# Putting a mixture of experts' results together: the gather split between the last expert and the end

## The chip, the cores and the metric

The kernel is one program on one core of a Trainium2 chip. The metric is the device time of one execution in microseconds (us). TensorE (PE) does the matrix products, VectorE (DVE), ScalarE (ACT) and GpSimd (Pool) work on data in the core's own memory, SyncE (SP) only issues transfers. All five run their own instruction streams and meet at semaphores; transfers run on 16 shared DMA engines.

## What is computed

Two layers over 2048 rows of 512 values. The change touches the end of the second one, a mixture of eight experts of which each row uses two:

```python
probs = softmax(xt @ gate_w.T)
top_vals, top_idx = top_k(probs, 2)
top_vals = top_vals / sum(top_vals)
act = silu(einsum('th,efh->tef', xt, w1)) * einsum('th,efh->tef', xt, w3)
expert_out = einsum('tef,ehf->teh', act, w2)
y = einsum('te,teh->th', w_full, expert_out)      # w_full holds the two top_vals of each row
...
g = silu(y)
x = x + s * g                                     # s: the second attention's message
```

The inputs are drawn from a fixed seed. Worked out from the reference, the eight experts get 515, 546, 493, 538, 524, 479, 477 and 524 rows.

## The kernel before

Four stages run one after the other, each a block of five instruction streams with a barrier between them: `first_stage` (weights and first gate), `attention`, `across_batch` (second attention, routing, and the sorting of rows by expert), `experts`, and then `combine`.

**Sorting.** In `across_batch` VectorE finds for every row its two experts and the two places (`s.slots`) that the row takes in a list sorted by expert, in which each expert starts on a multiple of 128. Pool then writes the rows to `rows_by_expert` (`s.xs`) with 32 indirect transfers (16 tiles of 128 rows, 2 places each, L1187). Places that no row takes stay zero: `attention` fills the whole list with zeros first (L1058). The last instructions of VectorE in this stage (L1339 to L1349) make small tables from the counts: which expert a block of 128 belongs to, when its weights are ready.

**Experts.** The sorted list has 39 blocks (`NBLK`), the most that can occur; with these counts 37 hold rows (5, 5, 4, 5, 5, 4, 4, 5 by expert) and the last two are empty but computed all the same. Each block is a step: its rows are turned (L1669), multiplied with two weight matrices (L1681), gated on ScalarE and VectorE (L1568, L1625), turned (L1692) and multiplied with the third (L1704, L1706). In step b PE also finishes block b-1. ScalarE takes the result out of the accumulator (L1580) and stores it to `results_by_row` (`s.ys`, L1582). Pool loads and converts the next expert's weights (L1073, L1093) into one of two places, for even and for odd experts; each place is free once the last block of the expert in it is done. After the last conversion Pool loads into the free place what the end needs, 16 transfers of 512 KB (L1536): the first layer's output `s.x1` and the message `s.messages`.

**Combine.** A stage of its own. For each of 16 tiles Pool gathers the 128 rows of the first and of the second expert (L1763, 32 in all; five tiles of space, so that from the sixth on it waits for `mixed`), ScalarE scales the first by its weight (L1795), VectorE scales and adds the second (L1782), ScalarE applies silu (L1803), VectorE multiplies by the message (L1777) and adds the first layer's output (L1778), SP stores the tile (L1809). ScalarE works one tile ahead.

What sets the order is the program text of each engine and the semaphores; there is no scheduler.

## Time and profile before

| | us |
|---|---|
| median of 3 runs | 1499.13 (1498.78 to 1500.48) |
| the profiled execution, own time | 1501.16 |
| its span (first to last instruction) | 1499.2 |
| from the end of the last matrix product (1442.4) to the end of the span | 56.8 |

Of the span PE is busy 90%, VectorE 47%, ScalarE 38%, Pool 41%. The row of PE in 40 slices of 37.5 us tells where it is not: in the first slice, in two or three slices around the middle (`across_batch`, from 750 to 880 us), and in the last two slices (`combine`). A group of instructions is named by its line in the kernel, the engine and the operation; "[... <-X]" behind a line of the timeline is how long the engine had been idle and what ended that.

### The profile page before, as it was taken

The page shows a single profiled execution, that of the slowest core. Times are in us where ns is not written, and L with a number is a line of the kernel's source. Part 1 is how long each engine was busy: PE and PEld are TensorE (multiplying, and loading weights), DVE is VectorE, ACT ScalarE, POOL GpSimd, SP SyncE. Part 2 cuts the span into 40 slices and gives each one's busy share as a digit, 9 for nine tenths or more (in the row PEclk, how much of TensorE's full clock was granted, in tenths as well). Part 3 has the DMA queues.
Part 4 walks back from the last instruction along what each step waited for, and adds up shares of the span by engine and source line. Part 5 has one row for each costly group of instructions (what it writes and reads, how often), then busy time and mean ns, then how long its engine had stood idle before and what let it go on. Part 6 is the DMA issues. An engine that isn't in the chain of part 4 may idle for free. (4 is left out here: it accounts for less than half of the span.)

```text
span 1499.2 us, 24968 instructions
## 1 busy us (share of the span) xinstructions
PE 1349.1 (90%) x7870; PEld 1149.3 (77%) x7871; DVE 699.4 (47%) x1617; ACT 565.9 (38%) x1775; POOL 615.0 (41%) x516
## 2 busy tenths in 40 slices
PE   6989899999999999999877579999999999999940
PEld 6934487878787878888547469999999999999930
DVE  6352376666676766666447332223222222232237
ACT  3421276655556656666534221212212111122124
POOL 0020155444444545454325445172662617451135
PEclk9889999999999999999878689999999999999985
DMA  8035720000000000000015566273772728555247
GB/s 290 1 84 143 277 93 15 15 14 14 14 14 14 14 25 17 14 14 15 7 58 177 195 225 187 99 247 109 238 243 96 268 72 289 171 169 182 72 126 258
DMA packets 67068, 171.47 MB, mean 114 GB/s; under 512 B 6448, under 2 KB 15040, under 8 KB 66704
## 3 DMA queue, kind: packets, MB, share of 16 engines
q0 software_dynamic: 25776, 98.73, 19.9%
q1 hardware_dynamic: 35632, 61.95, 12.9%
q10 hardware_dynamic: 5616, 10.23, 1.9%
q8 instruction: 25, 0.41, 0.1%
q14 instruction: 19, 0.16, 0.0%
HBM read 125.26 MB, written 45.61 MB: 114 GB/s over the span
## 5 line engine op out<-in xcount | busy, mean ns | idle before, releaser
L1681 PE MATMUL bank<-expert_weights,rows_t 128*128 x1872 | 359.4, 347 | 1.8 <-DVE rows_t L1613 1.6
L1681 PEld LDWEIGHTS bank<-expert_weights,rows_t 128*128 128x128 f32 x1872 | 340.8, 189 | 5.8 <-issue 2.6
L958 ACT ACTIVATE room<-bank,room 128x256 f32<-128x256 f32 (+1 forms) x512 | 208.9, 415 | 114.0 <-DVE room L891 113.9
L986 POOL TENSOR_TENSOR room<-room 128x1024 f32<-128x1024 f32 (+1 forms) x128 | 187.9, 1468 | 120.1 <-DVE room L868 120.1
L742 PE MATMUL bank<-room 96*128 (+2 forms) x1024 | 189.1, 327 | 0.0
L1625 DVE TENSOR_TENSOR x_keep<-x_keep,bank 128x400 f32<-128x400 f32 x78 | 44.5, 571 | 304.2 <-ACT x_keep L1568 302.9
L1093 POOL TENSOR_TENSOR expert_weights<-x_keep,expert_weights 128x1600 fp32r<-128x1600 f32 (+2 forms) x49 | 160.2, 3270 | 54.9 <-DMA expert_weights<-w 54.6
L742 PEld LDWEIGHTS bank<-room 96*128 96x128 f32 x1024 | 159.1, 191 | 13.7 <-issue 0.4
L1704 PE MATMUL bank<-expert_weights,act_t 128*128 x702 | 165.6, 389 | 1.0 <-ACT act_t L1573 1.0
L993 POOL TENSOR_TENSOR room<-room 128x256 f32<-128x256 f32 x128 | 93.2, 728 | 173.5 <-DVE room L932 172.2
L1704 PEld LDWEIGHTS bank<-expert_weights,act_t 128*128 128x128 f32 x702 | 131.5, 188 | 25.6 <-issue 1.3
L1568 ACT ACTIVATE x_keep<-bank 128x400 f32<-128x400 f32 x78 | 39.3, 504 | 295.1 <-PE bank L1681 295.1
L891 DVE TENSOR_REDUCE room<-bank 128x4 f32<-128x1024 f32 (+1 forms) x128 | 120.9, 945 | 8.3 <-PE bank L742 8.3
L753 PE MATMUL bank<-ident_sb,room 128*128 128x128 f32 x768 | 116.5, 276 | 7.2 <-POOL room L986 3.7
L753 PEld LDWEIGHTS bank<-ident_sb,room 128*128 128x128 f32 x768 | 92.3, 141 | 32.6 <-issue 23.6
L709 PE MATMUL bank<-wq_parts,q_latent_parts 128*128 128x384 f32 x384 | 101.6, 373 | 5.8 <-DVE room L932 3.1
L781 PE MATMUL bank<-wo_parts,out_latent_parts 128*128 128x512 f32 x384 | 95.4, 405 | 8.1 <-DVE room L932 6.6
L958 ACT ACTIVATION_READ_ACCUMULATOR room<-bank,room 128x1 f32 x512 | 102.3, 200 | 0.0
L781 PEld LDWEIGHTS bank<-wo_parts,out_latent_parts 128*128 128x128 f32 x384 | 72.4, 192 | 29.5 <-issue 12.0
L907 DVE COPY probs_t<-bank 128x512 f32<-128x512 f32 x128 | 86.9, 679 | 4.7 <-PE bank L753 4.7
L930 DVE TENSOR_TENSOR room<-bank,consts_sb 128x384 f32<-128x384 f32 x128 | 70.4, 550 | 35.0 <-PE bank L709 34.9
L975 ACT ACTIVATE room<-bank 96x512 f32<-96x512 f32 x128 | 75.0, 586 | 26.2 <-PE bank L722 26.2
(231 smaller groups left out, 1773.4 us busy)
## 6 DMA issues: line engine op xcount, KB each, us to landing
x_keep<-w POOLq DMA_DIRECT2D x28, 800.0 KB, 5.0
expert_weights<-w POOLq DMA_DIRECT2D x28, 800.0 KB, 6.5
x_keep<-w POOLq DMA_DIRECT2D x14, 768.0 KB, 6.0
expert_weights<-w POOLq DMA_DIRECT2D x14, 768.0 KB, 7.7
rows_by_expert<-room SPq DMA_DIRECT2D x1, 9984.0 KB, 29.0
x_keep<-rows_by_expert SPq DMA_DIRECT2D x39, 256.0 KB, 4.0
results_by_row<-x_keep ACTq DMA_DIRECT2D x39, 256.0 KB, 4.6
room<-wo SPq DMA_DIRECT2D x16, 512.0 KB, 5.8
```

What stands on the lines that cost most here:

```text
L709: last = nc.tensor.matmul(psum(6)[:, 0:4 * KC], qs[:, of_q, qt], Wq[:, of_w, 4 * KC * u:4 * KC * (u + 1)], start=(i == 0), stop=(i == 2))
L742: last = nc.tensor.matmul(ps[:, w * hh:w * hh + w], QT[0:KC, qt, h], s.KT[0:KC, ds(b * SEQ, w)], start=False, stop=True, skip_group_check= ...
L753: last = nc.tensor.transpose(psum(5 - kt)[:, P * hh:P * hh + P], Pr[:, m % 4, hh, P * kt:P * kt + P], ident)
L781: last = nc.tensor.matmul(psum(6), OT[:, of_o, P * i:P * i + P], s.Wo[:, of_w, i], start=(p == 0 and i == 0), stop=(p == 2 and i == 7))
L891: v.tensor_reduce(nb[:, par], scores_bank(m)[:, 0:4 * w].rearrange("p (h k) -> p h k", h=4), AX.X, ALU.max, negate=True).then_inc(bias_rea ...
L907: v.tensor_copy(PT[:, pt_slot(two[1], 0)], psum(5)).then_inc(p_out, 1)
L958: last = sc.activation(Pr[:, m % 4, hh, 0:w], scores_bank(m)[:, w * hh:w * hh + w], ACT.Exp, bias=nb[:, par, hh:hh + 1], accum_out=sm[:, p ...
L986: g.tensor_tensor(pr, pr, rs[:, one[1] % 2].unsqueeze(2).broadcast_to([P, 4, w]), ALU.mult).then_inc(normed, 1)
L993: nc.gpsimd.tensor_tensor(q, q, qrot[:, m % 2], ALU.add).then_inc(q_added, 1)
L1093: return s.nc.gpsimd.tensor_tensor(low, raw, high, ALU.subtract)
L1681: last = mm(psum(2 * hf + w)[:, 0:HF], xgT[:, par, of_x, P * k:P * k + P], W[:, ds(off + (of_w * SLOT + (k * 2 + w) * FF + hf * HF), HF)], ...
L1704: mm(psum(7), actT[:, of_a, P * t:P * t + P], W[:, ds(off + (of_w * SLOT + W13 + t * D), D)], start=(i == 0 and t == 0), stop=False)
```

## The change

- The two places of a row are now kept in rising order: `slots[..., 0]` is the smaller, so the expert of lower number, `slots[..., 1]` the higher. The two weights are swapped to match, with eight small instructions on VectorE at the end of `across_batch`; five more work out how many stores of results must have landed before the last expert starts and when it ends (`s.landed`).
- `combine` is gone; its work stands at the end of the `experts` block. After converting the last expert's weights, Pool waits until the results of blocks 0 to 31 have landed, gathers the lower expert's rows of all 16 tiles (none of them can be the last expert), and loads the message. Then it waits until the results of block 36 have landed and gathers the higher expert's rows into sixteen separate places, made of what is left of the free weight place, the staging space and row buffers.
- ScalarE scales the lower rows, six tiles before the last block's result and the others one per tile. VectorE does three passes per tile as before.
- The first layer's output is no longer loaded early by Pool. SP loads it tile by tile, four tiles ahead of its use, between the stores of the output.
- `results_by_row` is now filled with zeros too, in `attention`, right behind the other list: another transfer of 9984 KB. Pool waits for both before it sorts.
- The semaphores of `first_stage` are given back and used again; Pool clears 46 of them at the start of `attention`.

Pool's stream from its last conversion on, at the end of `experts` (and in `combine` before); `late` is the free weight place, `room`, `kept` and `x_keep` are other space, a name behind "waits" is a semaphore. Before:

```order
L1093 TENSOR_TENSOR expert_weights<-x_keep,expert_weights 32x512 [waits high_in0,raw_in0]
L1529 TENSOR_LOAD tables
L1529 ISA x2
L1536 DMA kept<-x_after_layer 128x2x512 [waits y_done]
L1536 DMA kept<-layer_attention 128x2x512
...
L1757 UNCONDITIONAL_BRANCH [waits barrier_Pool_Activation_PE_DVE_SP_gather]
L1763 DMA room<-results_by_row,tables 128x512 x10
L1763 DMA room<-results_by_row,tables 128x512 [waits mixed]
L1763 DMA room<-results_by_row,tables 128x512
```

Now:

```order
L1107 TENSOR_TENSOR expert_weights<-x_keep,expert_weights 32x512 [waits lora_scaled,raw_in0]
L1590 TENSOR_LOAD tables
L1590 ISA x2
L1590 TENSOR_LOAD tables [waits y_stored0]
L1590 ISA x2
L1595 DMA late<-results_by_row,tables 128x512 [waits y_stored1]
L1595 DMA late<-results_by_row,tables 128x512 x15
L1603 DMA late<-layer_attention 128x2x512 x8
...
L1595 DMA late<-results_by_row,tables 128x512 [waits y_stored1]
L1595 DMA late<-results_by_row,tables 128x512 x6
L1595 DMA x_keep<-results_by_row,tables 128x512 x8
L1595 DMA x_keep<-results_by_row,tables 128x512 [waits rows_turned]
```

The barrier between the stages is gone from this stream, sixteen gathers stand ahead of the last blocks, and none of the other sixteen waits for VectorE.

ScalarE's stream around the last block's result. Before, where the results of the last block are followed by the barrier:

```order
L1803 ACTIVATE room<-room 128x512 [waits mixed]
L1795 ACTIVATE room<-room,tables 128x512 [waits c_done,rows_got1]
L1803 ACTIVATE room<-room 128x512 [waits mixed]
L1795 ACTIVATE room<-room,tables 128x512 [waits c_done,rows_got2]
L1803 ACTIVATE room<-room 128x512 [waits mixed]
```

Now, with the last block's result (L1671) and its store in the middle:

```order
L1664 ACTIVATE act_t<-bank2 128x512 [waits act_turned]
L1697 ACTIVATE late<-late,tables 128x512 [waits lower_in]
L1697 ACTIVATE late<-late,tables 128x512 x5
L1671 ACTIVATE x_keep<-bank3 128x512 [waits y_stored0,y_done]
L1673 DMA results_by_row<-x_keep 128x512 [waits y_out]
L1697 ACTIVATE late<-late,tables 128x512
L1707 ACTIVATE late<-late 128x512 [waits higher_added]
```

The scaling of six tiles moved ahead of the last result, and the first silu (L1707) stands behind it.

VectorE's stream for one tile in the new tail (`k_ready` and `silu_done` are numbers used again, here the landing of a gather and of a load):

```order
L1766 SCALAR_TENSOR_TENSOR late<-x_keep,tables,late 128x512 [waits k_ready,lower_scaled]
L1774 TENSOR_TENSOR late<-late 128x512 [waits c_gated]
L1777 TENSOR_TENSOR late<-late 128x512 [waits silu_done,c_done]
```

against before:

```order
L1782 SCALAR_TENSOR_TENSOR room<-room,tables 128x512 [waits scaled]
L1777 TENSOR_TENSOR room<-room,kept 128x512 [waits c_gated]
L1778 TENSOR_TENSOR kept<-kept,room 128x512 [waits c_dve]
```

The same three passes in the same order; only what they wait for has changed.

The core of the diff:

```diff
@@ build
-        s.kept = sb(ctx, "kept", [P, 2, NT, D])
+        s.first_place = sb(ctx, "late", [P, 2 * SLOT])
         experts(s)
-        s.room(sb(ctx, "room3", [P, 10000]))
-        combine(s)
@@ attention
             nc.gpsimd.memset(zeros, 0.0).then_inc(s.zeros_ready, 1)
+            for of_first_stage in s.done_with:
+                pool.sem_clear(of_first_stage)
...
             sp.dma_start(s.xs.rearrange("(n p) h -> p n h", p=P),
+                         zeros.unsqueeze(1).broadcast_to([P, NBLK, D])).then_inc(s.blank, 16)
+            sp.dma_start(s.ys.rearrange("(n p) h -> p n h", p=P),
                          zeros.unsqueeze(1).broadcast_to([P, NBLK, D])).then_inc(s.blank, 16)
@@ across_batch
-            v.tensor_copy(s.slots, slotf).then_inc(slots_ready, 1)
+            v.tensor_tensor(s.slots[:, :, 0], slotf[:, 0], slotf[:, 1], ALU.min).then_inc(slots_ready, 1)
+            v.tensor_tensor(s.slots[:, :, 1], slotf[:, 0], slotf[:, 1], ALU.max).then_inc(slots_ready, 1)
...
+            step(v.tensor_tensor(swap[:, 0], slotf[:, 0], slotf[:, 1], ALU.is_gt))
+            step(v.tensor_tensor(swap[:, 1], slotf[:, 0], slotf[:, 1], ALU.is_gt))
+            step(v.tensor_tensor(keep[:, 0], slotf[:, 0], slotf[:, 1], ALU.is_lt))
+            step.then(v.tensor_tensor(keep[:, 1], slotf[:, 0], slotf[:, 1], ALU.is_lt))
+            step(v.tensor_tensor(crossed[:, 0], ranked[:, 1], swap[:, 0], ALU.mult))
+            step(v.tensor_tensor(crossed[:, 1], ranked[:, 0], swap[:, 1], ALU.mult))
+            step.then(v.tensor_tensor(keep, ranked, keep, ALU.mult))
+            step(v.tensor_tensor(ranked, keep, crossed, ALU.add))
+            step(v.tensor_copy(until[:, 0:1], starts[:, E - 1:E]))
+            step.then(v.tensor_tensor(until[:, 1:2], starts[:, E - 1:E], n_blocks[:, E - 1:E], ALU.add))
+            step.then(v.tensor_tensor(below, until.unsqueeze(2).broadcast_to([P, 2, NBLK + 1]),
+                                      const("by_parity").unsqueeze(1).broadcast_to([P, 2, NBLK + 1]), ALU.is_gt))
+            step.then(v.tensor_reduce(n_below, below.rearrange("p i (r n) -> p i r n", r=2), AX.X, ALU.add))
+            step(v.tensor_scalar(s.landed, n_below, 16.0, 16.0, ALU.mult, ALU.add))
@@ experts, Pool
+            blocks_landed(0)
+            for t in range(NT):
+                bring_rows(z[:, t], t, 0, lower_in)
             for q in range(NT // 2):
-                pool.wait_ge(y_done, NBLK - NT // 2 + q)
-                for i, rows in enumerate((s.x1, s.messages)):
-                    pool.dma_start(s.kept[:, i, 2 * q:2 * q + 2],
-                                   rows[2 * P * q:2 * P * q + 2 * P, :].rearrange("(t p) n -> p t n", p=P)).then_inc(
+                pool.dma_start(S[:, 2 * q:2 * q + 2],
+                               s.messages[2 * P * q:2 * P * q + 2 * P, :].rearrange("(t p) n -> p t n", p=P)).then_inc(
+                                   s.kept_in, 16)
+            pool.wait_ge(s.converted, 1 + (E - 1) * NCH)
+            blocks_landed(1)
+            for t in range(NT):
+                if t == NT - 1:
+                    pool.wait_ge(x_turned, NBLK)
+                bring_rows(higher[t], t, 1, higher_in[t])
@@ experts, SP
+            for t in range(NT):
+                if t + X1 < NT:
+                    sp.wait_ge(summed, t + 1)
+                    sp.wait_ge(x1_in[t % X1], 16 * (t // X1 + 1))
+                    bring_x1(t + X1)
+                sp.wait_ge(done, 2 * t + 2)
+                sp.dma_start(s.out[P * t:P * t + P, :], z[:, t]).then_inc(stored, 16)
@@ experts, ScalarE
+            act.wait_ge(lower_in, 16 * NT)
+            for t in range(SCALED_FIRST):
+                scale(t)
             result(NBLK, 1, False)
+            for t in range(NT):
+                if t + SCALED_FIRST < NT:
+                    scale(t + SCALED_FIRST)
+                act.wait_ge(summed, t + 1)
+                sc.activation(z[:, t], z[:, t], ACT.Silu).then_inc(gated, 1)
@@ experts, VectorE
+            add_higher(0)
+            for t in range(NT):
+                if t + 1 < NT:
+                    add_higher(t + 1)
+                dve.wait_ge(gated, t + 1)
+                v.tensor_tensor(z[:, t], z[:, t], S[:, t], ALU.mult).then_inc(done, 1)
+                dve.wait_ge(done, 2 * t + 1)
+                dve.wait_ge(x1_in[t % X1], 16 * (t // X1 + 1))
+                v.tensor_tensor(z[:, t], z[:, t], x1_at[t], ALU.add).then_inc(done, 1)
```

## Rows read from the trace of the kernel before

**Rows 1.** The page: the chain that ended last, by line, in shares of the span.

```profile
POOL room L1763 2%; DMA room<-results_by_row,tables 1%; DVE room L1782 0%; DVE kept L1778 0%; DVE room L1777 0%; ACT room L1795 0%; POOLq L1756 0%; PEldq L1756 0%
```

**Rows 2.** A stretch: length, PE, PEld, DVE, ACT, POOL busy, PE clock, DMA share, GB/s.

```profile
1440.00:1499.20 59.20, 2.39 (x11) 1.65 (x9) 32.64 (x48) 20.56 (x33) 33.35 (x32) 0.56 0.70 217
```

**Rows 3.** Timeline, last block and first tile: start, length, engine, line, [idle before].

```profile
1437.04 0.60 ACT L1573 ACTIVATE act_t<-bank 128x512 fp32r<-128x512 f32 x1 [0.43 <-PE bank L1692]
...
1438.73 0.29 DVE L1637 TENSOR_TENSOR act_t<-bank,act_t 32x128 fp32r<-32x128 f32 x1
...
1442.42 0.60 ACT L1580 ACTIVATE x_keep<-bank 128x512 f32<-128x512 f32 x1 [4.78 <-PE bank L1706]
1443.05 0.35 ACTq L1582 DMA_DIRECT2D results_by_row<-x_keep  x1
1446.24 1.03 POOL L1763 DMA_INDIRECT room<-results_by_row,tables  x1 [22.39 <-PEq L1756]
...
1451.10 0.72 ACT L1795 ACTIVATE room<-room,tables 128x512 f32<-128x512 f32 x1 [8.08 <-DMA room<-results_by_row,tables]
```

**Rows 4.** The end's instructions by line: duration in ns min/median/max, first, last start.

```profile
L1763 POOL DMA_INDIRECT room<-results_by_row,tables x32: 942/1022/1467, 1446.2 to 1488.0; - x32
L1795 ACT ACTIVATE room<-room,tables x16: 721/722/722, 1451.1 to 1492.6; 128x512 f32<-128x512 f32 x16
...
L1803 ACT ACTIVATE room<-room x16: 612/612/631, 1454.4 to 1494.1; 128x512 f32<-128x512 f32 x16
```

**Rows 5.** Timeline, the last tiles on VectorE.

```profile
1493.35 0.75 DVE L1782 SCALAR_TENSOR_TENSOR room<-room,tables 128x512 f32<-128x512 f32 x1
1494.02 0.69 DVE L1777 TENSOR_TENSOR room<-room,kept 128x512 f32<-128x512 f32 x1
...
1494.74 0.69 DVE L1778 TENSOR_TENSOR kept<-kept,room 128x512 f32<-128x512 f32 x1
1495.35 0.68 DVE L1777 TENSOR_TENSOR room<-room,kept 128x512 f32<-128x512 f32 x1
1496.07 0.69 DVE L1778 TENSOR_TENSOR kept<-kept,room 128x512 f32<-128x512 f32 x1
```

**Rows 6.** Timeline: Pool's last conversion; the stores of blocks 31 and 36.

```profile
1329.95 4.74 POOL L1093 TENSOR_TENSOR expert_weights<-x_keep,expert_weights 128x1536 fp32r<-128x1536 f32 x2 [1.98 <-DMA expert_weights<-w]
...
1351.70 0.35 ACTq L1582 DMA_DIRECT2D results_by_row<-x_keep  x1
...
1422.81 0.36 ACTq L1582 DMA_DIRECT2D results_by_row<-x_keep  x1
```

**Rows 7.** Transfers issued from 1350 to 1352: count, KB, us to landing.

```profile
results_by_row<-x_keep ACTq DMA_DIRECT2D x1, 256.0 KB, 2.4
```

**Rows 8.** Timeline: the start of attention on Pool; and a register instruction's ns.

```profile
167.25 0.52 POOL L1037 MEMSET room<- 128x512 f32 x1 [83.29 <-POOLq L286]
169.83 0.73 POOL L993 TENSOR_TENSOR room<-room 128x256 f32<-128x256 f32 x1 [2.06 <-DVE room L932]
...
L1706 PEldq FUSED_REGOPS  x18: 46/46/46, 1203.3 to 1439.3; - x18
```

**Rows 9.** Timeline: the small table instructions at the end of across_batch.

```profile
798.72 0.17 DVE L1285 TENSOR_TENSOR room<-room 128x16 f32<-128x16 f32 x1
798.93 0.25 DVE L1286 RECIPROCAL room<-room 128x16 f32<-128x16 f32 x1
...
875.57 37.91 SPq L1543 DMA_DIRECT2D x_keep<-rows_by_expert  x6
```

**Rows 10.** Timeline: ScalarE and PE at the end of Pool's scatter.

```profile
849.85 0.60 ACT L1229 ACTIVATE room<-bank 128x512 f32<-128x512 f32 x1 [20.33 <-remote]
...
850.50 3.78 PE L1431 MATMUL bank<-room 128*128 128x128 f32 x16 [11.28 <-ACT room L1229]
```

**Rows 11.** The page's transfers, and SP's next load after the zeros.

```profile
rows_by_expert<-room SPq DMA_DIRECT2D x1, 9984.0 KB, 29.0
...
239.33 0.36 SPq L1045 DMA_DIRECT2D gate_tiles<-gates  x1
```

137 lines of the change are left out of this document (67 added, 70 removed).

## The prediction, made before the change was run

> **What bounds the kernel now.** I read the page first. The chain of work that ended last lies wholly in the combine stage: Pool's gathers L1763, transfers, and a little of each pass on VectorE and ScalarE [rows 1]. Then the table by stretch: in the last 59.2 us PE works 2.39 us, VectorE 32.64, ScalarE 20.56, Pool 33.35, and the DMA engines 0.70 of the time at 217 GB/s [rows 2]. So everything behind the last matrix product is an end of its own, and PE, which sets the pace before it, is not in it. The timeline shows how it starts: ScalarE takes out the last result from 1442.42 to 1443.02, the first gather begins at 1446.24 behind the barrier, and the first tile reaches ScalarE only at 1451.10 [rows 3]. From there 32 gathers follow from 1446.2 to 1488.0 [rows 4]: (1488.0 - 1446.2) / 31 = 1.35 us each, 2.7 us per tile. VectorE needs less: in the one place where it works without a wait, the starts of the passes lie 0.67 (L1782 to L1777), 0.72 (L1777 to L1778, which depends on it) and 0.61 us (L1778 to the next) apart [rows 5], 2.00 us per tile. ScalarE needs 0.72 + 0.61 = 1.33 us [rows 4]. **Pool's issue of gathers bounds the end, VectorE is next.** The last pass ends at 1496.07 + 0.69 = 1496.76 [rows 5] and the span at 1499.2: 2.44 us for the last store.
>
> **The gathers of the lower rows.** Pool is free from 1329.95 + 4.74 = 1334.7 [rows 6]. Block 31's results are issued at 1351.70 [rows 6] and such a store lands in 2.4 us [rows 7], so 16 gathers of 1.35 us run from about 1354.5 to 1376, and eight message loads behind them. This lies beside PE's steps with 80 us to spare. Its cost beside PE I put at nothing; what it is if that cover is gone is the slower rival below. What also goes from this time are eight transfers of 512 KB for the first layer's output, which waited for nobody.
>
> **The gathers of the higher rows.** They wait for block 36, not for the last block: by the counts of the reference the last two of the 39 blocks hold no rows. Block 36's store is issued at 1422.81 [rows 6] and lands near 1425.5; with two table reads on Pool I start at 1426.5. Sixteen gathers of 1.35 us are issued by 1448. The first tile needs its rows at 1439, the last at about 1473, so none is late. If all 39 blocks held rows they would start near 1446, land by 1451 and cost some 5 us; that is a matter of the data and I leave it at zero.
>
> **What is late next.** VectorE finishes its work for the last block at 1438.73 + 0.29 = 1439.02 and ScalarE the same at 1437.64 [rows 3]. ScalarE then scales six tiles (about 0.63 us from start to start, 0.72 the last): until 1441.5. VectorE adds two higher tiles and stops, since the first silu stands on ScalarE behind the last block's result. That result waits for PE until 1442.42, its store is issued until 1443.40 [rows 3], one more scaling takes 0.63 and silu 0.61: 1444.7. Here VectorE starts and does not stop again if nothing else is late: 16 tiles of 0.72 + 0.61 for the two last passes and 14 remaining first passes of 0.67 are 21.3 + 9.4 = 30.7 us, to 1475.4. With the same 2.44 us for the last store the span would end at 1477.8. The gain of the end is **1499.2 - 1477.8 = 21.4 us**. ScalarE's 1.33 us per tile hides behind VectorE's 2.00. SP's load of the first layer's output for tile t+4 is issued when tile t-1 is done, some 10 us before use. The transfers per tile are 256 KB in and 256 KB out per 2.0 us, 262 GB/s. The end of before moved 217 GB/s on average at a DMA share of 0.70 [rows 2], which at a full share would be 310. That is close, but below it; only the last gathers, until about 1450, come on top.
>
> **Costs elsewhere.** (1) VectorE, end of across_batch: 13 small instructions more. Starts of such instructions are 0.21 us apart when the second waits for the first [rows 9], and I take 0.09 without that wait (the 0.17 us of a duration less the 0.08 of overlap that the 0.75 us pass shows against its 0.67 us step in [rows 5]). Six wait at 0.21 to 0.27, seven do not: 6 x 0.23 + 7 x 0.09 = 2.0; I take **1.9 us**. They are in full on the path: SP loads the first rows at 875.57 [rows 9] as soon as VectorE lets the barrier go. (2) One instruction more ahead of the sorting: 0.1 us. (3) Pool clears 46 semaphores between its memset, ended at 167.77, and its first sum at 169.83, where it had been idle 2.06 us [rows 8] and where PE takes up the sum at once. No row shows what clearing costs. From below: nothing, if 46 of them fit into the 2.06 us (up to 45 ns each); from above, 0.30 us each, the pause between two of Pool's gathers (1.35 less their median 1.02), which makes 13.8 - 2.06 = 11.7 us. The nearest row in kind is a register instruction of 46 ns on PE's sequencer [rows 8]: 2.1 us, over the idle time by less than 0.1. I take **0.3**. (4) The second fill with zeros: the first takes 29.0 us [rows 11] from shortly after the memset's end at 167.77 [rows 8], the second would last until about 227, and SP's next load is at 239.33 [rows 11]. Nothing waits for it before the sorting, over 500 us later: zero.
>
> Of (3) the Trainium skill has a figure: "Runtime: NRT & Kernel Launch", section Instruction fetch mechanics, gives a sequencer some 20 cycles per instruction as the least, and "Advanced Engine Details and Errata", Clock Domains, 1.2 GHz for Pool's. An estimate from these pages is 46 x 20 / 1.2 GHz = 0.8 us, well inside the idle time, and the sum would be 0.3 us less; no run here shows it yet.
>
> **The sum.** -21.4 + 1.9 + 0.1 + 0.3 = -19.1 us. Against the profiled execution's span of 1499.2 this is 1480.1, its own time 1501.16 would be 1482.1. The profiled execution lies 2.0 us above the median of the runs, 1499.13, so for the median I forecast **1480 us**, a ratio of 0.987. A difference of under 0.2%, 3 us, is about what a measurement of this kernel can't tell from none.
>
> **Rivals.**
> *A, late code or transfers in the end (+10 us, 1490).* In the sorting stage ScalarE stood 20.33 us and PE 11.28 us, both until Pool's 32 scatters were through [rows 10], with nothing named that they waited for: something that each engine needs came late while Pool's indirect transfers ran. In the new kernel the second run of gathers, 1426.5 to 1448, lies over PE's last product and the start of the tail. If the last result came only behind these gathers, first silu would move from 1444.7 to about 1454, and the end with it: +10. For it speaks that row; against it that in the combine stage of before 32 gathers ran in an even 1.35 us each with ScalarE and VectorE busy 20.56 and 32.64 us beside them [rows 2, 4], with no stop of 10 us. If the DMA engines were the bound, at 217 GB/s instead of 262, 7.3 MB from 1444.7 on would take 34 us instead of 31: a milder form, +3. Chance 0.17.
> A rule of the Trainium skill speaks against A: "Runtime: NRT & Kernel Launch", Instruction fetch mechanics, has the fetch of code running ahead on a queue of its own and mostly hidden while code runs in sequence. By it A would have no price and the time would stay at 1480; the standing engines in rows 10 are why I don't drop it.
> *B, clearing semaphores is dear (+9, 1489).* The upper bound of (3). Pool's first sum would start up to 11.7 us late, and PE turns it at once, so the whole of attention moves. Chance 0.07.
> *C, the sorting stage moves.* The standstill there depends on where code and transfers meet, and both have shifted by an instruction or two. It can shrink or grow; its 11.28 us bound it both ways: 1469 to 1491, most likely within 5 of the forecast. Chance 0.10, half on each side.
> *D, slower (1503).* Both runs of gathers, each over 20 us, stop PE as the scatter did, by its 11.28 us each: 2 x 11.3 = 22.6, and 1480 + 22.6 = 1503. The place is Pool's gathers at 1354 and 1426 beside PE's steps. It decides from 19.1 us of standstill on. Against it: between the stores of blocks 31 and 36 a step took (1422.81 - 1351.70) / 5 = 14.22 us [rows 6] while Pool brought its 512 KB transfers beside it. Chance 0.05.
> *E, nothing of it (1499).* The change doesn't get its early start, because the wait for landed results holds Pool until the last block. Then 16 gathers (21.6 us) would still be all that stands behind 1443, below VectorE's 31; only the first landing, 5 us, is added: 1485. So even this is no zero. Chance 0.03.
>
> **How the numbers follow.** The forecast, 1476 to 1484, has 0.58. A 0.17, B 0.07, C 0.10, D 0.05, E 0.03. To hold 8 in 10 the range takes in A and B and the near half of C: **1475 to 1491**. Faster by over 0.2% (below 1496): all but D and a sum of A and B, **0.91**; within 0.2%: **0.03**; slower: **0.06**.
>
> **What the new profile would show.** Pool's lower gathers near 1356 (plus the 2.3 us by which all is later) and its higher ones from about 1428 to 1450; no gather behind it. VectorE without waits of over 0.1 us from about 1447 to 1478, 2.00 us per tile, and a chain that ended last made of VectorE's three lines alone. If instead VectorE waits for loads of the first layer's output, the DMA engines are the bound; if for silu, ScalarE. At the start, Pool's first sum at 169.8 to 170.3; every us beyond is B. SP's first load of rows 2 us later against the end of the last store of messages. Steps of 14.2 us on PE between 1354 and 1450 speak against A and D. Wrong altogether would be a VectorE pass that is slower on its new places: 0.1 us more per pass is 4.6 us.

## The result, and the profile after

The changed kernel took **1505.17 us** (median of 5 runs, 1503.72 to 1508.21) against 1499.63 us of the kernel before in the same comparison (1498.78 to 1501.53): a ratio of 1.004, with a 95% interval of 1.0029 to 1.0051. It is slower by 5.5 us where 1480 was forecast, and outside the forecast range of 1475 to 1491. Its profiled execution has a span of 1503.4 us, against 1499.2 before.

The end behaves as forecast. This is the timeline of the kernel after: ScalarE's last result, and where VectorE takes up its 14th and 15th tile (start, length, engine, line, operation, in brackets the idle time before it and what ended it).

```profile
1467.96 0.60 ACT L1671 ACTIVATE x_keep<-bank 128x512 f32<-128x512 f32 x1 [3.56 <-PE bank L1827]
...
1495.48 0.75 DVE L1766 SCALAR_TENSOR_TENSOR late<-x_keep,tables,late 128x512 f32<-128x512 f32 x1
...
1497.47 0.74 DVE L1766 SCALAR_TENSOR_TENSOR late<-x_keep,tables,late 128x512 f32<-128x512 f32 x1
```

From the start of the last result to the end of the span it is 1503.4 - 1467.96 = 35.4 us, before 1499.2 - 1442.42 = 56.8 [rows 3]: 21.3 us less. VectorE goes from tile to tile in 1.99 us (1495.48 to 1497.47) without a wait. So the time was lost ahead of the end. The next fence shows where: the two runs of gathers on Pool, and what ScalarE and TensorE (PE) do beside the first.

```profile
1353.66 1.03 POOL L1595 DMA_INDIRECT late<-results_by_row,tables  x1 [20.90 <-DMA results_by_row<-x_keep]
...
1350.75 0.35 ACTq L1673 DMA_DIRECT2D results_by_row<-x_keep  x1
...
1368.01 0.50 ACT L1659 ACTIVATE x_keep<-bank 128x400 f32<-128x400 f32 x1 [11.93 <-remote]
1376.68 0.60 ACT L1671 ACTIVATE x_keep<-bank 128x512 f32<-128x512 f32 x1 [8.17 <-remote]
1377.45 0.35 ACTq L1673 DMA_DIRECT2D results_by_row<-x_keep  x1
...
1363.95 2.33 PE L1802 MATMUL bank<-expert_weights,rows_t 128*128 x10
1366.56 0.34 PE L1802 MATMUL bank<-expert_weights,rows_t 128*128 x1 [0.28 <-issue]
1367.99 0.43 PE L1802 MATMUL bank<-expert_weights,rows_t 128*128 x1 [1.09 <-issue]
...
1376.44 3.02 PE L1802 MATMUL bank<-expert_weights,rows_t 128*128 x8 [0.92 <-issue]
```

Sixteen gathers go out from 1353.66 on, the last at 1372.53. PE still goes on for 12.9 us. Then its matmuls come one by one, 1.4 or 2.1 us from start to start, with nothing in the profile that they wait for ("issue"), until 1376.44, 3.9 us behind the last gather. ScalarE waits 11.93 and 8.17 us for what the profile can only call "remote". These waits begin before PE slows down: the result that ScalarE takes out at 1376.68 was complete when PE's matmul of L1827 ended at 1364.12, by the trace, 12.6 us earlier. From the store of block 31 to that of block 32 it is 26.7 us (1350.75 to 1377.45), where a step of before took 14.22 [rows 6]. The higher rows do the same to the last two blocks:

```profile
1433.47 0.36 ACTq L1673 DMA_DIRECT2D results_by_row<-x_keep  x1
...
1459.07 0.60 ACT L1671 ACTIVATE x_keep<-bank 128x512 f32<-128x512 f32 x1 [14.43 <-remote]
...
1436.90 1.01 POOL L1595 DMA_INDIRECT late<-results_by_row,tables  x1 [57.56 <-issue]
...
1446.24 0.40 PE L1827 MATMUL bank<-expert_weights,act_t 96*128 x1
...
1459.83 0.42 DVE L1733 CAST act_t<-bank 128x256 fp32r<-128x256 f32 x1 [14.32 <-remote]
...
1460.88 6.81 PE L1825 MATMUL bank<-expert_weights,act_t 128*128 x18 [13.47 <-ACT act_t L1664]
```

Here no matmul is late. The one whose signal ScalarE waits for (L1827) ends at 1446.64, and ScalarE starts at 1459.07, 12.4 us behind it. VectorE's cast at 1459.83 waits for transposes of PE that ended at 1447.41, also 12.4 us earlier. PE meanwhile waits for what ScalarE makes of these transposes. So what comes late in this run is what PE signals, for work that the trace shows as done. The last gather is issued at 1455.77, 3.3 us before it is over.

The table by stretch (length; busy time of PE, PE's weight loads, VectorE, ScalarE, Pool; PE clock, DMA share, GB/s) says how much PE does beside the first run, between the runs, beside the second, and right behind it:

```profile
1353.70:1376.40 22.70, 15.08 (x73) 12.40 (x72) 3.76 (x9) 2.13 (x4) 18.13 (x21) 0.87 0.71 210
1377.00:1434.00 57.00, 57.00 (x304) 53.76 (x303) 15.07 (x36) 11.28 (x21) 2.34 (x4) 0.97 0.27 97
1436.90:1459.10 22.20, 10.51 (x59) 9.42 (x57) 3.11 (x8) 1.63 (x4) 15.24 (x16) 0.85 0.66 190
1460.80:1464.00 3.20, 3.12 (x7) 2.51 (x8) 2.70 (x5) 3.20 (x6) 0.00 (x0) 0.50 0.96 307
```

Between the runs PE is busy 57.00 of 57.00 us; beside them 15.08 of 22.70 and 10.51 of 22.20. When PE goes on behind the second run, after standing for 13.47 us, its granted clock is 0.50, the lower of its two levels (1.2 GHz). The 18 matmuls of the last product then take 6.81 us, where the same 18 of the block before take 4.24 at a clock of 1.00. That is how 12.4 us of late signals become 14.9. The chain that ended last, as far as the profile can follow it, now lies on PE for 37% of the span.

Put together, from landmark to landmark (differences to the kernel before in us):

| stretch | before | after | difference |
|---|---|---|---|
| start to Pool's memset of attention [rows 8] | 167.25 | 163.52 | -3.7 |
| to the first load of rows for the last experts [rows 9] | 708.32 | 713.20 | +4.9 |
| to the store of block 31 [rows 6] | 476.13 | 474.03 | -2.1 |
| to the store of block 36 [rows 6] | 71.11 | 82.72 | +11.6 |
| to the last result on ScalarE [rows 3] | 19.61 | 34.49 | +14.9 |
| to the end of the span | 56.78 | 35.44 | -21.3 |

The 26.5 us of the fourth and fifth row are the first and the second run of gathers, and they are more than the 21.3 that the end gives back. The first three rows together are -1.0.

### The profile page after: what moved, and what is told of

Read it like the earlier page. It is cut to its first block and busy times, and to the rows that moved or that the text cites. A ratio compares the mean times of both kernels' runs of the same rounds, so it can differ in the third digit from the quotient of the medians.

```text
span 1503.4 us, 25070 instructions
## 1 busy us (share of the span) xinstructions
PE 1352.4 (90%) x7870; PEld 1152.7 (77%) x7871; DVE 700.1 (47%) x1631; ACT 565.4 (38%) x1775; POOL 604.7 (40%) x508
## 5 line engine op out<-in xcount | busy, mean ns | idle before, releaser
L1671 ACT ACTIVATE x_keep<-bank 128x512 f32<-128x512 f32 x39 | 23.3, 597 | 166.1 <-PE bank L1827 143.5
```

## The experiments

Unless it says otherwise, an edit is made on the kernel after. Executions of one kernel lie up to 11 us apart, largely by what happens before the last expert (the same result of one block came at 1359.63 in one of these kernels and at 1353.68 in the next, with the same code up to there), so where one profiled execution is read, it is read by lengths of steps and not by its span. Ratios are to the kernel before, run beside; where no ratio is given, the time is that of a single execution.

### Lower rows one at a time

```
             for t in range(NT):
+                if t >= 1:
+                    pool.wait_ge(lower_in, 16 * t)
                 bring_rows(z[:, t], t, 0, lower_in)
```

> The changed kernel, but each of the 16 gathers of the lower expert's rows waits until the one before it has landed; they then take about 4.5 us each and fill the time from 1354 to 1427. Theory 1 (what PE signals comes late only while Pool's indirect transfers follow each other without a pause, at 1.25 us): the step in which they lay, 26.7 us, returns to 14.2 and the whole loses its 12 us of standstill, so about 1493 us by the median of the changed kernel, 1505. Theory 2 (every indirect transfer beside PE costs PE a fixed share, about 12 us / 16 = 0.7 us each): the loss is only spread, steps of 16 us or so, and the time stays at 1505. The second run of gathers is left as it is, with its 14.9 us.

Measured: 1492.26 us (1490.79 to 1497.98), ratio 0.9943 (0.9926 to 0.9959). ScalarE's results and the first gathers in the trace of this kernel:

```profile
1359.63 0.60 ACT L1673 ACTIVATE x_keep<-bank 128x512 f32<-128x512 f32 x1 [3.90 <-PE bank L1829]
1373.89 0.60 ACT L1673 ACTIVATE x_keep<-bank 128x512 f32<-128x512 f32 x1 [3.90 <-PE bank L1829]
...
1363.31 1.03 POOL L1595 DMA_INDIRECT late<-results_by_row,tables  x1 [19.91 <-DMA results_by_row<-x_keep]
1367.06 0.97 POOL L1595 DMA_INDIRECT late<-results_by_row,tables  x1 [2.72 <-DMA late<-results_by_row,tables]
...
1460.71 0.60 ACT L1673 ACTIVATE x_keep<-bank 128x512 f32<-128x512 f32 x1 [9.94 <-remote]
```

With a gather every 3.7 us the step is 14.26 us (1359.63 to 1373.89): the first standstill is gone, with the same 16 gathers beside the same products. The second one, beside the higher rows, is still there (9.94 us). So it is the run back to back that costs, not a gather beside PE.

### Higher rows behind the last result

```
             blocks_landed(1)
+            pool.wait_ge(y_done, NBLK + 1)
```

> The changed kernel, but the gathers of the higher expert's rows start only when PE's last product is done, so that this run lies beside no work of PE. Both theories: the last block's result comes 14.9 us earlier, at about 1453 instead of 1468; the first tile then waits for its rows (about 5 us after that), and VectorE's 32 us follow. 1468 + 35.4 becomes 1453 + 5 + 0.7 + 32.6 + 2.4 = 1494 in span, so about 1495 us, 9 less than the changed kernel. If VectorE and ScalarE stand still beside the gathers too (theory 3: every engine is hit, not just what PE signals), tiles would be held up by 10 us or more and the time is 1505 or above.

Measured: 1499.49 us (1492.85 to 1503.76, 10 runs), ratio 0.9986 (0.997 to 1.0002); expected were 1495, just below the 1495.8 to 1500.6 that this interval makes of 1500.30. A part of the time was lost ahead of the edit: in the profiled execution block 31's result came at 1356.77, 6.8 us later than in the kernel after. The lower run stops its step as before; behind the last result the sixteen gathers go out back to back:

```profile
1356.77 0.60 ACT L1672 ACTIVATE x_keep<-bank 128x512 f32<-128x512 f32 x1 [3.90 <-PE bank L1828]
1383.61 0.60 ACT L1672 ACTIVATE x_keep<-bank 128x512 f32<-128x512 f32 x1 [4.01 <-remote]
...
1460.44 0.60 ACT L1672 ACTIVATE x_keep<-bank 128x512 f32<-128x512 f32 x1 [1.12 <-PE bank L1828]
...
1464.64 0.75 DVE L1767 SCALAR_TENSOR_TENSOR late<-late,tables 128x512 f32<-128x512 f32 x1 [7.62 <-DMA late<-results_by_row,tables]
```

VectorE gets its first tile 4.2 us behind the last result and then keeps 1.99 to 2.00 us per tile beside the run. In this end VectorE passes three instructions for a tile, ScalarE two, and neither is held up.

### Both

> Both edits together. Theory 1: 12 us from the first and 9 to 10 from the second, about 1483 us, below both kernels (before 1499.6, changed 1505.2). Theory 2: only the second edit counts, about 1495. Theory 3: about 1493 to 1505.

Measured: **1483.31 us** (1481.37 to 1486.5), ratio 0.9882 (0.9866 to 0.9899), against an expected 1483. Steps are 14.26 us throughout and the last result starts at 1445.10. Taking the two runs out of PE's way brings back nearly the whole forecast: 1505.2 less 1483.3 is 21.9 of the 26.5 us lost, and of the missing 4.6 some 4 are the wait for the first higher rows behind the last result (39.6 us from the last result to the end of the span, where it was 35.4).

### Plain transfers in the place of the lower gathers

```
-                bring_rows(z[:, t], t, 0, lower_in)
+                pool.dma_start(z[:, t], s.ys[P * t:P * t + P, :]).then_inc(lower_in, 16)
```

The lower rows that reach a tile are then those in order, not the tile's own.

> The changed kernel, but the first run of 16 gathers is 16 plain transfers of the same size, 256 KB, from the same list in order, issued back to back on the same queue (the rows that reach a tile are then not its own). If it is the indirect form of a transfer (Pool reading indices and writing descriptors one row at a time) that holds up what PE signals, the step of 26.7 us returns to 14.2 and the span is about 1491. If it is the amount and rate of data on Pool's queue, or on the DMA engines as a whole, the standstill stays and the span is about 1503.

Measured: 1496.78 us. Sixteen transfers of the same 256 KB from the same queue, in a row:

```profile
L1601 POOL DMA_DIRECT2D late<-results_by_row x16: 538/538/581, 1356.8 to 1364.8; - x16
...
1353.38 0.60 ACT L1671 ACTIVATE x_keep<-bank 128x512 f32<-128x512 f32 x1 [3.89 <-PE bank L1827]
1367.63 0.60 ACT L1671 ACTIVATE x_keep<-bank 128x512 f32<-128x512 f32 x1 [3.89 <-PE bank L1827]
```

They are issued in 8.5 us, more than twice as fast as gathers, and the step is 14.25 us. The same bytes at a higher rate don't stop PE; the indirect form does. A run of direct transfers that lasts as long as the 18.9 us of the gathers was not tried, but eight gathers in 9.8 us, hardly longer than these 8.5, do hold ScalarE up (see the next section). This is the row that the prediction lacked: it had argued from direct transfers.

### Bursts of four, of eight, and half rows (each with the higher rows behind the last result)

```
             for t in range(NT):
+                if t and t % 4 == 0:
+                    pool.wait_ge(lower_in, 16 * t)
                 bring_rows(z[:, t], t, 0, lower_in)
```

> As high_late, but the lower gathers go in bursts of four, each burst waiting until all before it have landed. In the changed kernel what PE signalled first came late some 6 us after a run of gathers had begun, so it may take a length of run. If it does: four gathers at 1.25 us are 5 us, with a pause of some 3 us for the last to land, and no step is longer than 14.3 us. If gathers one behind the other hurt from the first on, each of the four bursts costs some 2 to 3 us, steps of 16 to 17 us.

> The same with bursts of eight, 10 us of gathers without a pause. If a length of run is what counts and it is near 6 us: about 4 us late per burst, so two of the steps near 18 us. If the number of gathers counts, the loss is as with bursts of four.

> As high_late, but the 16 lower gathers in a row take half a row each (256 values, 1 KB, so the same number of indices and rows with half the bytes); the other half of each tile, filled with the same first halves, follows one at a time. If Pool's making of the transfers row by row holds up PE's signals, the step still takes about 26 us while the 16 run. If the bytes moved do, the stop is gone or halved (14.3 to 20 us).

Measured: 1488.14, 1486.43 and 1495.09 us. The time alone would not tell four from eight; the waits on ScalarE do. First the two rows of bursts of eight, then of sixteen gathers of half a row each:

```profile
1365.55 0.51 ACT L1662 ACTIVATE x_keep<-bank 128x400 f32<-128x400 f32 x1 [9.20 <-remote]
1378.33 0.51 ACT L1662 ACTIVATE x_keep<-bank 128x400 f32<-128x400 f32 x1 [7.39 <-remote]
```

```profile
1372.26 0.50 ACT L1668 ACTIVATE x_keep<-bank 128x400 f32<-128x400 f32 x1 [15.51 <-remote]
1378.85 0.60 ACT L1680 ACTIVATE x_keep<-bank 128x512 f32<-128x512 f32 x1 [6.09 <-remote]
```

With bursts of four no wait is "remote", and the steps are 14.26 us. Bursts of eight hold ScalarE up twice, by 3.8 us over the three steps in question (46.6 for 42.8). Half the bytes per gather stop it as long as whole rows do: the two steps concerned take 40.4 us for 28.5, 11.9 more, where whole rows cost 11.6. So the length of a run counts, and the size of its gathers does not. Whether length means the number of gathers or the time that they last is not separated: half rows too are issued 1.25 us apart.

### Free work on PE beside the higher run

On the kernel "both": 192 transposes of the identity behind PE's last product, twelve for each tile, which wait for nothing; ScalarE's silu of a tile waits for its twelve.

```
             down(NBLK - 1, place(NBLK - 1))
+            for t in range(NT):
+                for k in range(12):
+                    last = tr(psum(t % 2)[:, P * (k % 4):P * (k % 4) + P], ident, ident)
+                last.then_inc(pe_beside, 1)
```

> The kernel with both edits, whose end ran its 16 gathers back to back beside VectorE and ScalarE at 2.00 us per tile without a wait. Added: behind its last product PE transposes the identity 12 times per tile (about 1.6 us) and signals, and silu of a tile waits for that signal too. If it is what PE signals that comes late beside such gathers, the end stops: ScalarE waits up to 12 to 15 us for PE until the gathers are through, and the span grows from 1484.7 to about 1495. If only the experts' steps are hit for another reason (their loads, their weights), PE stays ahead and the span stays within 2 us of 1485.

Measured: 1496.81 us. PE in this trace, whose sixteen gathers are issued from 1446.21 to 1465.51, and ScalarE's fifth tile:

```profile
1445.77 8.57 PE L1873 MATMUL bank<-ident_sb 128*128 128x128 f32 x77
...
1459.92 0.37 PE L1873 MATMUL bank<-ident_sb 128*128 128x128 f32 x1 [2.58 <-issue]
...
1469.08 14.32 PE L1873 MATMUL bank<-ident_sb 128*128 128x128 f32 x104 [0.71 <-issue]
...
1469.17 0.63 ACT L1712 ACTIVATE late<-late 128x512 f32<-128x512 f32 x1 [11.50 <-remote]
```

This is the disputed cost by itself. Nothing that PE reads, writes or waits for depends on the gathers, and still it does 77 transposes in 8.57 us (its stop begins 8.1 us behind the first gather), eleven in the next 14.7, and the other 104 in one stretch that starts 3.6 us behind the last gather. The late signals of the kernel after are here too: the twelve transposes of ScalarE's fifth tile are among the 77, the last of them ended at 1452.48, and ScalarE takes the tile up at 1469.17, 16.7 us later.

### The same, gathers in bursts of four

> The control to "pe_tail": the same 192 transposes on TensorE behind its last product, with nothing that they wait for, and the higher gathers in bursts of four that wait for their landing. The transposes take 0.11 us each as in the first 8.57 us of "pe_tail", 21 us in all, so ScalarE's tiles never wait for them if TensorE runs freely. Theory 1 (the run back to back slows TensorE's own issue): TensorE goes through the 192 without single matmuls apart, and four gathers take 4 x 1.25 + 3.3 us, a tile every 2.1 us against VectorE's 2.0, so the time is 1484 to 1488. Theory 2 (any indirect transfer beside TensorE slows it, or the transposes themselves cost the end): gaps of 1 to 2.6 us as in "pe_tail", 1495.

Measured: 1495.92 us, where 1484 to 1488 was expected. The part on PE is as theory 1 has it, the time is not:

```profile
1445.19 21.13 PE L1876 MATMUL bank<-ident_sb 128*128 128x128 f32 x192
...
1454.96 1.34 POOL L1596 DMA_INDIRECT late<-results_by_row,tables  x1 [4.52 <-DMA late<-results_by_row,tables]
```

PE does all 192 without a gap. But Pool's bursts start 9.3, 10.2 and 11.7 us apart and not the 8.3 that I had put in, since each lands later here, where the loads and stores of the end run beside it; VectorE then waits for rows. Where rows are needed every 2 us, bursts are the wrong remedy, and gathers behind PE's work are the right one.

### Three higher gathers early

On "both": the first three higher gathers are issued beside the last products, each when the one before has landed, the other thirteen behind the last result.

```
             for t in range(NT):
+                if 1 <= t <= 3:
+                    pool.wait_ge(higher_in[t - 1], 16)
+                if t == 3:
+                    pool.wait_ge(y_done, NBLK + 1)
```

> As in "both", each gather of the lower rows waits until the one before has landed; but of the higher gathers the first three no longer wait for the last result (y_done): they go out beside the last expert's last products, each waiting until the one before has landed, and the other thirteen wait for the last result. Theory 1 (it is the run of outstanding indirect transfers that holds up what TensorE signals, not an indirect transfer as such): three gathers one at a time cost TensorE nothing, the first tiles lie there when the last result is written, and the end loses the wait from the last result to the first landed higher row, about 3.7 us of "both": about 1480. Theory 2 (any indirect transfer of the higher rows beside these last products holds TensorE up by 0.5 us or more each): the gain is eaten, 1483 or more. Theory 3 (the end is bound by the gathers' own pace of 1.3 us each or by VectorE's 2.0 us per tile with a start that other work sets): between the two, 1482.

Measured: 1480.92 us (1479.05 to 1485.98), ratio 0.9877 (0.9852 to 0.9903). It is near the 1480 of theory 1, but its interval covers that of "both", so the gain of 3.7 us is shown by the trace and not by the comparison: VectorE's first multiplication in the end now starts at 1446.17, 2.3 us behind the last result at 1443.87; in "both" it was 6.0 us (1451.13 and 1445.10).

### The scatters of the sorting stage

The kernel before had this standstill too, in a place that the change does not touch: ScalarE 20.33 us and PE 11.28 us beside 32 scatters in a row [rows 10]. In "early_three" PE shows the same picture there, single matmuls 1.40 us apart until 4.9 us behind the last scatter:

```profile
842.41 0.96 POOL L1203 DMA_INDIRECT rows_by_expert<-x_keep,tables  x1 [0.30 <-issue]
...
839.57 0.37 PE L1448 MATMUL bank<-ident_sb,room 128*128 128x128 f32 x1 [2.43 <-issue]
840.97 0.37 PE L1448 MATMUL bank<-ident_sb,room 128*128 128x128 f32 x1 [1.03 <-issue]
...
847.27 0.80 PE L1448 MATMUL bank<-ident_sb,room 128*128 128x128 f32 x3 [1.03 <-issue]
```

On "early_three", with 4 in one kernel and 6 in another:

```
             for t in range(NT):
                 for k in range(2):
+                    if t and (2 * t + k) % 4 == 0:
+                        pool.wait_ge(sorted_, 16 * (2 * t + k))
                     nc.gpsimd.indirect_dma_start(
```

> "early_three" with the pacing at a third place, the 32 indirect scatters of the tokens' rows beside the last steps of the sort and of the attention's second part: they go out in bursts of four, each burst waiting until all four before have landed. In the trace of "early_three" the run of 32 lasts from 801.53 to 843.4; TensorE then issues single matmuls about 1.4 us apart and ScalarE waits 7.93 and 22.94 us; two steps of 5.35 us each are done between 816 and 848, so about 21 us are lost there. Theory 1 (a run of indirect transfers back to back holds TensorE up, whatever its direction): the standstill goes; eight bursts of 4 x 1.27 plus about 3 us of landing end at about 866, and the last expert's loads start there instead of at 878.8: 12 us less, about 1469. Theory 2 (scatters are not like gathers, and the standstill there has another cause, such as the weights' loads): the standstill stays, and the scatters end later besides: 1481 or more.

> The same with bursts of six. Five bursts of 6 x 1.27 + 3 us and a rest of two end at about 858. Theory 1 with a limit on the number back to back between four and eight, as "burst_four" (no stop) and "burst_eight" (waits of 9.2 and 7.4 us) showed: if six are under it, the loads start at about 858 to 862, 1463 to 1469; if over it, TensorE still slows in each burst and the time is above that of bursts of four. Theory 2: 1481 or more.

Measured: **1472.65 us** (1470.11 to 1475.05), ratio 0.9821 (0.979 to 0.9852), and 1473.04 us (1469.3 to 1478.88), ratio 0.9823 (0.9782 to 0.9864). SP's first load of rows, in "early_three" and then in the kernel with bursts of four:

```profile
878.79 4.14 SPq L1622 DMA_DIRECT2D x_keep<-rows_by_expert  x3
```

```profile
867.36 12.95 SPq L1624 DMA_DIRECT2D x_keep<-rows_by_expert  x4
```

The load comes 11.4 us earlier, although the last scatter is issued 19 us later (861.39 instead of 842.41). Forecast were 12 us and 1469. Bursts of six gave no more: their scatters are through 2 us earlier, but ScalarE has two longer "remote" waits again, 2.8 and 4.5 us, and the stage ends at the same 867.5. So spacing removes the standstill for writing as for reading. The kernel with bursts of four is the fastest of this study, with that of six too near to tell apart: **27.5 us or 1.8% less than before** (1500.16 us in that comparison), 32 less than the changed kernel.

### What is held up: three engines, few or many instructions

The next four separate whether it is PE, its signals, or the number of instructions that an engine passes. Each is made on "both". In the first two the transposes of "pe_tail" are replaced by multiplications of 512 columns, three for each tile, and in the second of them `1 + t % 2`:

```
+            for t in range(NT):
+                for k in range(3):
+                    last = mm(psum(t % 2), ident, S[:, t], start=True, stop=True)
+                last.then_inc(pe_beside, 1)
```

> "pe_tail" with 48 matmuls of 512 columns in the place of the 192 transposes of 128, three per tile of the end, the same 16 signals to ScalarE, the same run of sixteen higher gathers back to back. Theory N (held up is what TensorE does per instruction: it comes to a stop after some 62 to 75 matmuls, as in four traces): 48 stay under that, TensorE goes through them without single matmuls apart, and ScalarE never waits for it longer than they take; the time is that of "both", 1484 to 1487. Theory H (beside such a run everything that TensorE signals is late, after some 9 us, whatever it executes): its signals from the fourth tile on come late again, ScalarE stands until the last gather is out, and the time is 1495 as in "pe_tail".

> "pe_tail" with 24 multiplications of 512 columns, 48 matmuls in the trace of 0.43 us each by "pe_tail_long", one and two by turns for each tile of the end: 20.6 us, as long as the 192 transposes take when nothing holds them, and a tile is free every 1.29 us, ahead of VectorE's 2.0. Theory N (what is held up goes by the number of instructions an engine has gone through beside such a run; 48 are under the 62 to 75 matmuls of the four traces): ScalarE never waits for TensorE, 1484 to 1487. Theory H (TensorE's signals come late by themselves beside such a run, as they seemed to in "pe_tail_long" from the fifth tile on): ScalarE waits several us for a signal whose matmuls are long done, until the last gather is out at about 20 us behind the last result, and the time is 1493 to 1496.

Measured: 1494.18 and 1489.09 us.

```profile
L1874 PE MATMUL bank<-late,ident_sb x96: 590/592/593, 1446.3 to 1487.1; 128*128 128x512 f32 x96
```

That is the first one, and it shows the error in its design: a multiplication of this kind is two matmuls, 96 of them, 0.43 us from start to start, so that the tiles are free every 2.57 us and the end is set by PE. Its time says nothing about the question. Its timeline shows the late signals again: PE has no gap, yet ScalarE's fifth tile starts at 1461.03 and its sixth at 1468.11, 1.7 and 6.2 us behind the end of the matmuls that they need. The second one answers a part of the question:

```profile
1446.84 20.76 PE L1874 MATMUL bank<-late,ident_sb 128*128 128x512 f32 x48
...
1457.12 0.63 ACT L1712 ACTIVATE late<-late 128x512 f32<-128x512 f32 x1 [0.74 <-issue]
1459.11 0.63 ACT L1712 ACTIVATE late<-late 128x512 f32<-128x512 f32 x1 [0.74 <-issue]
```

PE is as busy as with the 192 transposes and as long, beside the same sixteen gathers, but passes a quarter of the matmuls. It has no gap, and ScalarE never waits for it: its tiles follow at 1.99 us. This does not show that its signals are on time. The matmuls of the fifth tile end at 1453.01 and ScalarE takes it up at 1459.11, when VectorE is ready, so signals up to 6.1 us late would not be seen, as those of "pe_tail_long" would not have been. But the 16.7 us of "pe_tail", for a tile ready at the same time (1452.48), are ruled out: with fewer and longer matmuls there is neither the gap nor that delay. (The time is 2 us over the expected 1487: in this execution the last result came at 1447.04, 1.9 us later than in "both", and two tiles of VectorE took 0.6 us longer. Neither is a wait for PE.)

The other two put small instructions on VectorE (240 copies of one column ahead of its first tile) and on ScalarE (120 activations of one column ahead of its first silu), with nothing on PE:

> "both" with 240 copies of one column (128x1) on VectorE between the last result and the first tile of the end, beside the run of sixteen higher gathers; TensorE has nothing to do there. Such small instructions follow each other 0.08 to 0.09 us apart in the sorting stage, so they take about 20 us, and the end starts some 16 us later: about 1500. Theory N for every engine (an engine that goes through more than some 130 instructions beside such a run is held up): gaps of 0.7 to 2 us between single copies after the first 120 to 150, until the last gather is issued, and 1503 or more. Theory T (TensorE alone): no gaps, 240 in one stretch of about 20 us.

> "both" with 120 activations of one column (128x1) on ScalarE between the first summed tile (some 5 us behind the first higher gather) and the first tile's SiLU, beside the same run of gathers; nothing on TensorE. At 0.1 to 0.2 us apart they take 12 to 24 us. Theory N for every engine: after the first ones, gaps of 0.7 to 1.4 us between single activations, as on VectorE, until the last gather is issued some 20 us behind the last result; the time is then at least 1484.7 plus 16, 1500 or more. Theory V (only TensorE and VectorE): one stretch without gaps, 12 us at 0.1 us apart: about 1497.

Measured: 1505.64 and 1507.79 us. VectorE, whose gathers are issued from 1440.28 to 1459.16:

```profile
1440.12 5.18 DVE L1767 COPY bank<-ident_sb 128x1 f32<-128x1 f32 x84 [3.50 <-PE bank L1833]
...
1461.64 0.16 DVE L1767 COPY bank<-ident_sb 128x1 f32<-128x1 f32 x1 [0.53 <-issue]
1462.34 0.16 DVE L1767 COPY bank<-ident_sb 128x1 f32<-128x1 f32 x1 [0.54 <-issue]
1463.04 6.21 DVE L1767 COPY bank<-ident_sb 128x1 f32<-128x1 f32 x101 [0.54 <-issue]
```

And ScalarE, whose gathers are issued from 1446.50 to 1465.39:

```profile
1451.25 4.33 ACT L1712 ACTIVATE bank<-ident_sb 128x1 f32<-128x1 f32 x44 [3.25 <-DVE late L1772]
...
1468.99 3.25 ACT L1712 ACTIVATE bank<-ident_sb 128x1 f32<-128x1 f32 x34 [0.54 <-issue]
```

Both engines slow down to a few instructions every 1.4 us and are free again 3.9 and 3.6 us behind the last gather, as PE was. So it is not something of PE's. **Beside a long run of indirect transfers an engine that passes many instructions is held, after a first stretch, to a few every 1.4 us until the run is over**; an engine that passes few long instructions shows no such gap. The first stretch is not one fixed number: 64 to 66 matmuls in 11.9 to 12.6 us in the traces of "after", "high_late" and "low_half", 77 in "pe_tail", 84 copies in 5.2 us on VectorE, 44 activations on ScalarE that began 4.8 us behind the first gather.

What remains open is which part of the chip this is. The transfers that the profile lists as instruction queues are few (in "dve_small" one at 1442.9 and one at 1464.5, none between), so the code's own loads do not show what is late. A pure count of instructions does not explain the late signals: in the second run of the kernel after, 12.4 us late behind 59 matmuls, and in "pe_tail_long" behind 30 and 36. One rival is untested: every execution on record has a span and a granted clock, so each of them was recorded while it ran, and no run shows whether instructions and signals would also be late without the recording.

## Why the prediction was wrong, step by step

- **What bounds the end**, Pool's issue at 1.35 us per gather with VectorE's 2.00 us per tile next: right. VectorE takes 1.99 us, without a wait.
- **The gain of the end, 21.4 us**: right; 21.3 us from the last result on.
- **"Its cost beside PE I put at nothing": this is the step that failed.** The lower run cost 11.6 us, from the store of block 31 to that of 36. The reason given, 80 us to spare, was about whether the rows come in time, not about what a run does to its neighbours. The evidence given under rival D, steps of 14.22 us beside 512 KB transfers, was of direct transfers; "low_direct" shows that those are harmless in any case and say nothing of gathers.
- **The gathers of the higher rows, early and free**: the start was right in kind (1436.90, 3.4 us behind the store of block 36), the price was not: 14.9 us more from that store to the last result, of which 12.4 are late signals and 2.5 the last product at the lower clock. They are only free behind PE's work ("high_late", "both"), or a few of them spaced out ("early_three").
- **Rival A** is what happened in the second run: the last result came only behind its gathers, for +14.9 us instead of +10. The row for it [rows 10] was the right one, and I set against it that 32 gathers had run in the end of before without a stop. That fits the later runs: VectorE passed 48 and ScalarE 33 instructions in those 59.2 us [rows 2], where it took 84 and 44 in a few us to bring on a stop ("dve_small", "act_small"). The rule of the Trainium skill that I named against A (page "Runtime: NRT & Kernel Launch", Instruction fetch mechanics: code runs ahead on a queue of its own, mostly hidden) did not help here: VectorE's 240 copies stand in a plain sequence and were held up for 12.5 us all the same (the sum of the pauses between them). That does not refute the rule, since no run shows that it was the code that came late.
- **Rival D** is what happened: place, mechanism and, at 1503 against 1505.2, price. Its terms were 11.3 us per run; measured were 11.6 and 14.9. That they are so near is partly luck: the 11.28 us were one wait of PE beside 32 scatters, in a stage from which spacing later brought back 11.4 us, and nothing said that 16 gathers would cost the same. It had 0.05. Rows 10 were the only rows of a long run of indirect transfers beside PE, and they showed a stop; the nearest row deserved to be the likeliest case.
- **13 small instructions, 1.9 us**: right. In the trace of after they stand between 872.26 and 874.09: 1.83 us.
- **46 cleared semaphores, 0.3 us**: mis-sized by 0.5 us, which does not matter. Pool's first sum comes 2.88 us behind its memset instead of 2.06, so 0.8 us later, and a clear costs at most 2.88 / 46 = 63 ns. The attention stage as a whole is not longer for it (593.1 against 593.6 us). Rival B falls. By the estimate from the Trainium skill's pages, 0.8 us for all 46, the clears would have stayed inside the idle time; the row speaks for more, though it doesn't show what else may lie in the 2.88 us.
- **The second fill with zeros, nothing**: right, by the same stage's length.
- **Rival C**, the sorting stage moves: it did. ScalarE's wait there was 22.22 us instead of 20.33, and of the +4.9 up to the first load 3.6 are left when the small instructions (1.8) and a slightly shorter attention (-0.5) are taken off. It is the same kind of standstill, as "scatter_four" suggests, which removes it by spacing; whether its length moved for the reason that the rival gives was not tested.

## What to carry to other kernels

Long runs of gathers or scatters on Pool are not hidden by going out beside other engines' work: a run of sixteen back to back cost 12 to 15 us of PE's time, and 32 cost more than the 11 us that came back. Space them: let every fourth wait for the landing of those before, or let each wait for the one before where there is time. Put runs that must be fast where the other engines pass few instructions. When a stage stands still with releasers named "remote" or "issue", look for a run of indirect transfers that ends some 4 us before it does, and try the spacing first: it is a two-line edit. Compare the end of the instruction that signals with the start of the one that waits: here the first was done 12 us before the second began. A standstill of PE also costs clock behind it.

## What the runs showed of the hardware that I had not expected

- Beside a run of indirect transfers, PE stopped after 77 small transposes in 8.6 us, but passed 48 long matmuls in 20.8 us; VectorE stopped after 84 small copies, ScalarE after 44.
- Beside such a run ScalarE and VectorE took up finished work of PE late: 12.6 and 12.4 us in the kernel after, 16.7 us in "pe_tail", 1.7 and 6.2 us in "pe_tail_long".
- Behind the second standstill PE's granted clock was 0.50 (1460.80 to 1464.00), and 18 matmuls took 6.81 us instead of 4.24.
- While it lasts, instructions start at distances near multiples of 0.70 us (1461.64, 1462.34, 1463.04 on VectorE; 1.40 us on PE), and it ends 3.3 to 4.9 us after the last transfer's issue.
- Four gathers in a row left no wait (four scatters: waits of 0.7 and 2.3 us), six scatters: two waits of 2.8 and 4.5 us on ScalarE, eight gathers waits of 9.2 and 7.4 us. Half the bytes per gather made no difference, and sixteen direct transfers of 256 KB in 8.5 us did nothing.
- A gather alone lands 3.2 to 4.1 us after its issue beside PE's products ("low_one", "both"), but a burst of four beside the loads and stores of the end keeps Pool waiting 4.5 to 6.3 us ("pe_tail_four").
- A multiplication of f32 by 512 columns shows in the trace as two matmuls, 0.43 us from start to start ("pe_tail_long").
